# Two graph layers over one adjacency matrix: other segment lengths, a tail of 12 column blocks and not 16, and shorter beginning, epilogue and drain

## The reference, cut to what matters

```
deg = sum(adj, axis=1)
h   = relu(concat(x, (adj @ x + x) / (deg + 1)) @ W0 + b0)     # then each row / its 2-norm
x1  = layernorm(x + h)
n1  = adj @ x1 / (deg + 1)
out = layernorm(x1 + concat(x1, n1) @ W1.T)
```

## Time and profile before

| | before |
|---|---|
| runs | 763.28, 763.99, 767.74 us |
| the profiled execution's own time | 763.49 us |
| its span, first to last instruction | 761.7 us |
| busy share of TensorE matmul, weight load | 83%, 76% |
| busy share of VectorE, ScalarE, GpSimd | 91%, 77%, 37% |
| read from HBM | 270.6 MB |
| mean granted TensorE clock | 0.941 |

### The profile page before, as it was taken

How to read it: one execution, slowest core, us unless ns; L and a number is a source line. 1 busy time by engine, 2 the same in 40 slices (tenths; PEclk the granted TensorE clock), 3 DMA queues, 4 the chain that set the end, 5 groups by cost and what they waited for, 6 DMA issues and landing times.

```text
span 761.7 us, 27876 instructions
## 1 busy us (share of the span) xinstructions
PE 633.2 (83%) x11125; PEld 581.1 (76%) x11125; DVE 690.5 (91%) x2662; ACT 587.2 (77%) x815; POOL 283.8 (37%) x314
## 2 busy tenths in 40 slices
PE   0346788777778787889799898999999999998994
PEld 0346777676667676778788797989898989988994
DVE  2799987999898999999999999999999999988884
ACT  1978778999888898979889898888898888840032
POOL 0222212543222435345253634463543526331034
PEclk9987766999999999999999999999999999999998
DMA  9999999999999999999999999999999999900003
GB/s 361 384 368 393 421 367 421 421 419 420 418 419 421 416 419 417 404 418 405 421 405 421 405 419 404 419 408 403 404 397 419 409 417 406 411 14 2 3 19 100
DMA packets 41515, 274.53 MB, mean 360 GB/s; under 512 B 4454, under 2 KB 8614, under 8 KB 8614
## 3 DMA queue, kind: packets, MB, share of 16 engines
q1 hardware_dynamic: 39040, 270.55, 87.0%
q10 hardware_dynamic: 2342, 2.16, 0.9%
HBM read 270.60 MB, written 2.10 MB: 358 GB/s over the span
## 4 chain that ended last, share of the span: by engine, by line
PE 27%; DVE 26%; DMA 20%; issue 12%; ACT 9%; POOL 5%; ACTq 0%; DVEq 0%; SPq 0%
DMA a_in<-in_adj 18%; PE s_ps L383 14%; DVE e L792 7%; ACT junk L585 7%; DVE t_sb L799 6%; PE u_ps L402 4%; POOL small L1173 4%; DMA xl<-in_x 2%; DVE q_sb L866 2%; PE z_ps L450 2%; DVE y_sb L860 2%; PE p_ps L369 2%; PE p_ps L462 1%; DVE a_in L799 1%; DVE u_sb L799 1%
## 5 line engine op out<-in xcount | busy, mean ns | idle before, releaser
L585 ACT ACTIVATE junk<-a_in 128x2048 uint8<-128x2048 uint16 x256 | 488.9, 1915 | 10.4 <-DMA a_in<-in_adj 10.2
L383 PE MATMUL s_ps<-xh,t_sb 128*128 128x129 f16 x4096 | 390.2, 252 | 37.5 <-DVE t_sb L799 33.5
L383 PEld LDWEIGHTS s_ps<-xh,t_sb 128*128 128x128 fp8e4 x4096 | 315.3, 103 | 67.7 <-DVE t_sb L799 38.8
L792 DVE TENSOR_SCALAR e<-a_in 128x2048 uint8<-128x2048 f32 x256 | 311.0, 1222 | 12.5 <-DMA a_in<-in_adj 11.5
L1190 POOL COPY store<-pk 128x32 uint32<-128x32 uint32 (+1 forms) x250 | 203.2, 854 | 236.3 <-ACT pk L594 236.3
L799 DVE TENSOR_SCALAR t_sb<-pk 128x128 uint32<-128x128 uint32 x1024 | 152.0, 220 | 3.1 <-ACT pk L594 2.1
L369 PE MATMUL p_ps<-pow_h,e 128*128 128x16 f16 x2048 | 90.8, 171 | 68.8 <-DVE e L792 59.0
L1173 POOL TENSOR_TENSOR small<-small,minus_half 128x4 f32<-128x4 f32 x32 | 70.0, 2187 | 196.8 <-DVE small L854 149.7
L369 PEld LDWEIGHTS p_ps<-pow_h,e 128*128 128x128 f16 x2048 | 77.9, 99 | 83.1 <-DVE e L792 70.2
L402 PE MATMUL u_ps<-xh,u_sb 128*128 128x64 f16 x2976 | 105.6, 192 | 0.0
L402 PEld LDWEIGHTS u_ps<-xh,u_sb 128*128 128x128 fp8e4 x2976 | 100.4, 97 | 1.3
(11 more groups left out here) (119 smaller groups left out, 465.0 us busy)
## 6 DMA issues: line engine op xcount, KB each, us to landing
a_in<-in_adj SPq DMA_DIRECT2D x256, 1024.0 KB, 11.5
xl<-in_x ACTq DMA_DIRECT2D x4, 512.0 KB, 18.3
out_h<-e SPq DMA_DIRECT2D x8, 256.0 KB, 2.2
b_sb<-in_L_gnn_b ACTq DMA_DIRECT2D x3, 0.2 KB
w_sb<-in_L_gnn_W ACTq DMA_DIRECT2D x1, 32.0 KB
w_raw<-in_L_gnn_W ACTq DMA_DIRECT2D x1, 32.0 KB
```

The costliest lines, as they stand in the source:

```text
L383: last = nc.tensor.matmul(s_ps[:, n % 2, at:GW], t_sb[:, b // 2, b % 2::2], xh[:, b, at:GW], start=(b == 0), stop=False)
L585: nc.scalar.activation(junk[:, t % 2, :], halves[t % R], ACT.Copy, scale=1.0 / 128, accum_out=half_sum[:, n, c:c + 1]).then_inc(s_half, 1)
L792: nc.vector.tensor_scalar(e8[:, c, :], a_in[:, t % R, :], 1.0, float(CODE), ALU.is_equal, ALU.add).then_inc(s_e, 1)
```

## The change

1. `START` is 0, 12, 16, 24, 32, 40, 48, 56 and not 0, 12, 20, 28, 36, 44, 52. `WIDTH` becomes 8, 4, 8, 8, 8, 8, 8, 12 blocks. The tail has the column blocks 52 to 63. `catch_up` has 3416 matmuls in all and not 2976; in the turns 48 to 63 it has 1632 and not 1168, in the turns before 48 it has 1784 and not 1808. Of the 4096 matmuls of `sum_quarter` 1620 are wide and not 1584.
2. Both tail passes take six column blocks (`TW`) in pairs of 64 columns: 96 matmuls for each of 16 groups, one add each. The tail's unpacked buffers are eight (`VR`) and not six.
3. Beginning: TensorE packs row block 0 ahead of the transposes of W1; `split_x` (x into its two parts) moves from turn 0 to turn 1 on ScalarE and VectorE, the copies of W1 on ScalarE to the end of turn 1, `weights` and `bias` on VectorE to turn 2, `guard_x` to the turns 3 to 6.
4. Epilogue: GpSimd adds the high and low parts (`join_x`, `join_g`) and copies the degree; VectorE's `mean` and `begin_acc` lose those instructions and wait for GpSimd; the squares of `norm` go to ScalarE, and VectorE keeps one reduction.
5. End: ScalarE finishes the groups 0 and 1 alone (`NA = 2`), VectorE the others; the flag is copied ahead of the last group's add; SyncE branches on the flag before it waits for the output DMAs.

The core of the diff:

```diff
-START = [0, 12, 20, 28, 36, 44, 52]
+START = [0, 12, 16, 24, 32, 40, 48, 56]
-NA = 4
+NA = 2
-VR = 6
+VR = 8
+TW = WIDTH[-1] // 2
...
+            pe.wait_ge(s_glo, (TAIL + TW + BR - 1) // BR)
             tail_sums(0)
...
             for n in range(NB):
                 e, k = n // BR - 1, n % BR
                 sum_codes(n, 0)
+                if n == 1:
+                    split_x(0)
                 if e >= 0 and k == 2:
                     take_z(e)
-                if n == 0:
-                    split_x(0)
...
-                                     ACT.Relu).then_inc(s_r, 1)
+                                     ACT.Relu).then_inc(s_relu, 1)
+                act.wait_ge(s_relu, e + 1)
+                nc.scalar.activation(q_sb[:, :, :], r_sb[:, :, :], ACT.Square).then_inc(s_r, 1)
...
-                link(nc.vector.tensor_copy(dcol[:, rows], agg[:, par, :, 2 * HP:GW].rearrange("p k o -> p (k o)")))
-                link(nc.vector.reciprocal(small[:, 0, :], dcol[:, rows]))
-                link(nc.vector.tensor_tensor(s_sb[:, :, :], agg[:, par, :, HP:HP + F], agg[:, par, :, HP + F:2 * HP],
-                                             ALU.add))
+                link(nc.vector.reciprocal(small[:, 0, :], agg[:, par, :, 2 * HP:GW].rearrange("p k o -> p (k o)")))
+                dve.wait_ge(s_xsum, e + 1)
...
-                for k in range(BR):
-                    ins = nc.vector.scalar_tensor_tensor(out=q_sb[:, k, :], in0=r_sb[:, k, :], scalar=1.0,
-                                                         in1=r_sb[:, k, :], op0=ALU.mult, op1=ALU.mult,
-                                                         accum_out=small[:, 1, k:k + 1])
-                link(ins)
+                link(nc.vector.tensor_reduce(small[:, 1, :], q_sb[:, :, :], AX_X, ALU.add))
...
+                if g == NV - 1:
+                    dve.wait_ge(s_badps, 1)
+                    nc.vector.tensor_copy(bad_i[0:1, 0:1], c_ps[0:1, 0, 0:1]).then_inc(s_flag, 1)
                 add_tail(NV + g)
...
+            def join_x(e):
+
+                pool.wait_ge(s_agg, (e + 1) * BR)
+                hi, lo = (agg[:, e % 2, :, HP + i * F:HP + (i + 1) * F] for i in range(2))
+                nc.gpsimd.tensor_tensor(hi, hi, lo, ALU.add).then_inc(s_xsum, 1)
...
+                    nc.gpsimd.tensor_tensor(hi, hi, lo, ALU.add)
+                nc.gpsimd.tensor_copy(dcol[:, e * BR:(e + 1) * BR],
+                                      agg[:, e % 2, :, 2 * HP:GW].rearrange("p k o -> p (k o)")).then_inc(s_dcol, 1)
```

More of the change, by code:

```diff
@@ L69 @@
 TAIL = low(NQ - 1)
[L70 removed]
+WIDTH = [low(s + 1) - low(s) for s in range(NQ - 1)] + [NB - TAIL]
+TW = WIDTH[-1] // 2
 ROWS = [START[s + 1] - 1 for s in range(NQ - 1)] + [NB]
@@ L80, in piece @@
     return j * ROWS[q - 1] // steps, (j + 1) * ROWS[q - 1] // steps
-PIECE = max(piece(n)[1] - piece(n)[0] for n in range(START[1], NB))
+PIECE = max((piece(n)[1] - piece(n)[0]) * WIDTH[seg(n) - 1] for n in range(START[1], NB))
 def turn(slot):
@@ L358, in _ @@
             if_bad(sp, general_sp)
+            for i in range(4):
+                sp.wait_ge(s_out[i], 16 * NV // 4)
         @block.tensor
@@ L513, in _ @@
             pe.wait_ge(s_pow, 1)
+            for c in range(NC):
+                pack_chunk(0, c)
             pe.wait_ge(s_w, 80)
@@ L518, in _ @@
             last.then_inc(s_w1t, 1)
-            pe.wait_ge(s_w1, 1)
-            for n in range(NB):
+            for n in range(1, NB):
                 e, k = n // BR - 1, n % BR
@@ L1215, in _ @@
                 e, k = n // BR - 1, n % BR
+                if e >= 0 and k == 1:
+                    join_x(e)
                 if e >= 0 and k == 2:
@@ L1221, in _ @@
                     own_rows(e)
+                if e >= 0 and k == 1:
+                    join_g(e)
                 if e >= 0 and k == 2:
@@ L1225, in _ @@
             own_rows(NE - 1)
+            join_x(NE - 1)
+            join_g(NE - 1)
             root(0, NE - 1)
```

98 lines of the change are left out of this document (48 added, 50 removed).

## The result

The changed kernel takes 766.85 us (median of 20 runs, 764.69 to 768.73) and the kernel before 763.97 (20 runs, 762.65 to 767.74). The ratio is 1.0041 with a 95% interval of 1.0032 to 1.0050: 3.1 us slower, 2.4 to 3.8. The forecast was +1.8 on the median, 765.8, inside 1%. Of the runs further down, one of half_catch_up_late took 1899.65 us and one of old_segments_and_epilogue 1983.60; their ratios leave these out, their medians do not (755.36 and 762.54 without them), and no trace shows the cause.

The account below looks back on a forecast made before the run. Transfers were taken to bound the middle, TensorE nearly the last turns; 13.8 + 0.2 - 2 - 6.7 - 0.8 - 2.4 = +2.1 us on 763.49 gave 765.6, named 765.8 for the median; range 757 to 773.

Parts of the forecast that it names:

- The sum: Whole kernel: 13.8 + 0.2 - 2 - 6.7 - 0.8 - 2.4 = +2.1 us on the profiled 763.49; 765.8 named.
- The signs named beforehand: Four turns 40 to 42 us before turn 48, about 43 in 51 to 54, over 45 last; last copy near 697.5.
- What bounds the kernel: Transfers set the middle, four turns in 41.13 us; TensorE has 0.48 us left in four last turns; the tail has no transfers.
- Rival A: Middle: VectorE, not the transfers, sets the pace, so its 1.3 us less per four turns gives 756 us; 12 in 100.
- Still the pace of the transfers: Last turns: four take 40.95 us, read as set by transfers, with TensorE busy for 40.47.
- Catch-up, +13.8 and +0.2: Turns 48 to 63: 15.7 us more TensorE work less 1.9 free, bounds 12.5 to 15.7; +0.2 for the last row sum.
- Tail: After the row sums: first pass -6.7 us (-5.5 to -8.5), second pass to last scaling -0.8 (-3 to +1).
- Epilogue, 0: Work moved to GpSimd and ScalarE: no change; VectorE loses 1.3 us in four turns, a join taken at 1 us.
- The cover: Middle: the 1.8 us VectorE has free in four turns hides its wait for GpSimd's join.
- Rival B: Epilogue: GpSimd's joins hold VectorE up, 1.3 us in each of ten groups, giving 779 us; 15 in 100.
- Beginning, -2: Start: first buffers come free sooner, -2 us (-6 to +4), all of it arriving at turn 48.
- Drain, -2.4: Last scaling to end: early flag, branches beside the last group and output DMA, -2.4 us (-1.5 to -3).

Follow-up runs that it names:

- half_catch_up_late: The changed kernel without the second matmul of each catch-up pair in turns 48 to 63 (816 of 1632 left out); 755.61 us, ratio 0.9904 to the kernel before.
- old_segments_and_epilogue: The kernel before with the new beginning and new drain alone, its segments, tail and epilogue kept; 762.60 us, ratio 0.9994.
- segments_undone: The changed kernel with the segment table and tail widths of before, all other edits kept; 762.75 us, ratio 0.9986 to the kernel before.
- segments_only: The kernel before with the new segment table and the tail of twelve blocks in 64-column pairs alone; 767.21 us, ratio 1.0051.

## Why the prediction came out right, point by point

**The number.** That it came inside 1% says little: twelve other versions timed here, whatever was taken out of them, lie between 0.9904 and 1.0076 too. The sum, +2.1, put on the median would have been 766.1; 765.8 was named, and 766.85 measured. The signs named beforehand did come: 43.2 us for the turns 52 to 55, 45.3 for the next four, a DMA share falling below 1, TensorE without idle time in the last turns; the last copy ended at 695.6 and not 697.5, and from there it was 68.0 us and not 66.

**What bounds the kernel.** Right for the middle as far as TensorE goes: half of its catch-up work there taken away gives nothing. Rival A, that VectorE sets the middle, no run puts to the test, for none takes much work from VectorE there: what the change was to take off came as 2.6 us and not 9.8. Against it speaks that VectorE waits for the transfers. It is idle for 16.8 us between 190 and 500 us in the changed kernel and for 15.3 before, and of that these waits are (in total, times, longest), first after, then before:

```profile
DVE e L799 <- DMA a_in<-in_adj: 10.0, 15, 1.3
```

```profile
DVE e L792 <- DMA a_in<-in_adj: 8.2, 18, 1.2
```

The forecast was wrong in a detail for the last turns. "Still the pace of the transfers" was read from a DMA share of 1.01. But those turns repeat to 0.01 us, 9.17, 9.52, 10.29 and 11.97, three times over, and the stretch from turn 48 on takes 173.4 to 173.7 us in each of the four traces with that code. Earlier the pace scatters: four turns take 40.57 to 41.67 us between 172 and 583 us. This is the chain of TensorE and VectorE, by chance as fast as the transfers, and an epilogue that only makes VectorE's unpackings late makes it 41.3 (segments_undone). The row itself said it: TensorE busy for 40.47 of 40.95, and the missing 0.48 is two waits for VectorE, 0.36 for an unpacking and 0.12 for a `compare`.

**Catch-up, +13.8 and +0.2.** The mechanism is shown by half_catch_up_late. The size is 12.8 for the segments (segments_only), at the low end of the 12.5 to 15.7: of the 15.7 us from prices TensorE's busy time shows 14.4, and of that 1.6 went into its idle time (2.8 us in this stretch before, 1.1 in segments_only), where 1.9 was forecast. Turn by turn the price holds where both kernels are full: 48 more catch-up matmuls and 4 more wide columns are 1.44 + 0.22 = 1.66, and 9.52 us became 11.18. The 13.6 of the trace has 0.9 of the epilogue in it.

**Tail.** -6.7 and -0.8 forecast; the segments give -6.5 and -1.1 (segments_only), and the epilogue takes 0.2 back in the first pass, the two scalings more on VectorE 0.43 in the second. 96 matmuls start 2.88 us apart, by the forecast's price.

```profile
715.59 3.05 PE L466 MATMUL s_ps<-xh,a_in 128*128 128x64 f16 x96
718.48 3.04 PE L466 MATMUL u_ps<-xh,a_in 128*128 128x64 f16 x96
```

**Epilogue, 0.** The step that failed in a small way, in two places. The cover was named for the middle, 1.8 us in four turns, and it held there. It was not asked who covers the two new waits in the turns 48 to 55 and in the tail: 0.87 + 0.23 = 1.1 us, of which the 0.87 are the later `pk`, twice 0.45. The price of `join_x` was fair; there are 16, with a mean of 1378 ns where 1 us was taken:

```profile
L1179 POOL TENSOR_TENSOR agg<-agg 128x256 f32<-128x256 f32 x16 | 22.1, 1378 | 66.8 <-ACT agg L606 66.8
```

In the tail, with VectorE in its wait, it takes 0.74 us. The Trainium skill, GPSIMD Engine Reference, section Elementwise, side-by-side cycle accounting, led to an estimate of 0.6 us; the trace has 0.73 at best and on the mean nearly twice that, so the measurement decides. Rival B does not occur: where VectorE waits for the join, it is 0.6 us and not the several that a price like that of the power would bring. The second place is the other direction. The forecast priced only what VectorE does to a join; that a join holds up an unpacking of VectorE by 0.55 us, twice in four turns, it did not ask, and that eats most of the 1.3 us. The row of 0.33 us was also misread: at 661.55 VectorE was in the midst of eight unpackings (660.88 to 662.09), not idle, so it takes more than a busy VectorE to make a copy last 6.17.

**Beginning, -2.** Wrong in what became of it. The gain at turn 4 is 2.4 us and more than the 2 taken, but "all of it arrives at turn 48" fails: 1.1 on the mean of the traces, 0.3 to 0.4 in the runs. ScalarE, said to begin at 16.03 us in either kernel, began at 15.48. The step took for granted that the transfers set the pace from 60 us on without a break, and between 100 and 140 us they did not. That the trace showed -3.9 here is mostly the scatter of turn 48.

**Drain, -2.4.** Wrong by 1.5 us. "Runs beside the last group" and "while the DMA is under way" was right for the engines, and missed that the branch brings a code fetch, which runs beside the last output and holds it up. That turned 1.8 us of waiting for the output into 2.2 and its landing from 2.1 to 3.6 us.

**The sum.** Two gains came short, 1.6 us at the beginning and 1.5 in the drain; the epilogue cost 1.1 in the late stretches and gave something back that is not located. Against that the segments cost about 4 to 5 us and not 6.5. So the total, 3.1 us for a forecast of 1.8, rests on errors of both signs that partly cancel: that it came so near is luck in part, while the two large terms, catch-up and first tail pass, were right in mechanism and in size.

## What to carry to other kernels

Work that leaves a short tail for the loop ahead of it is only won if the engine has room in those very turns: TensorE had 5.6 us free in four turns of the middle and 0.48 in the last ones, and every microsecond put there was paid. Ask of a hidden step for every stretch separately who hides it, the last full turns and the tail too. Work moved to another engine is not gone if the two hold each other up: look at the busy time of the engine that was to be relieved. And where turns repeat to a hundredth of a microsecond here, a chain of engines sets them, however full the transfers look.

## What the runs showed of the hardware

A branch over a large block of code costs TensorE's queue 3.4 to 3.9 us here, and 0.7 to 1.4 us after it comes a fetch of 16 KB, a single packet of 0.9 to 1.6 us. The last output, of 256 KB, lands after 2.7 to 3.7 us in the eight traces in which it meets this packet, after 2.5 to 2.6 in the two in which it meets only that of 8 KB, and after 2.1 in the four with a late flag.

An add of 128x256 on GpSimd beside VectorE takes 0.7 to 3.5 us. An unpacking of VectorE that starts beside it takes 0.76 to 0.79 us for 0.22.

A kernel's profiled execution differed from its median by up to 3.7 us, while the stretches from turn 48 to the last scaling repeated to a tenth in nearly all other traces of the same code: what scatters in the traces lies ahead of turn 48 and, by up to 1 us, in the drain.
